# One attention stage of a fused network: its output product cut in two halves, its unit table rewritten, one copy moved ahead of another

## The reference

```python
def _L2_xattn_ref(q, k, v, mask, Wq, Wk, Wv, Wo, bo):       # q = layernorm(x), k = v = ctx_1024
    qh, kh, vh = heads_split(q @ Wq), heads_split(k @ Wk), heads_split(v @ Wv)     # 16 heads of 64
    dots = jnp.einsum('bhid,bhjd->bhij', qh, kh) * 64 ** (-0.5)
    dots = jnp.where(mask[:, None, :, :], mask_value, dots)
    attn = jax.nn.softmax(dots, axis=-1)
    out = jnp.einsum('bhij,bhjd->bhid', attn, vh)
    out = out.transpose(0, 2, 1, 3).reshape(b, n, h * d)
    return out @ Wo + bo
...
    x = x + _L2_xattn_ref(_layernorm(x, axis=-1), ctx_1024, ctx_1024, mask_BxSxS2_bk1, ...)
```

## Time and profile before

| | |
|---|---|
| median of the timed runs | 2631.06 us |
| the profiled execution, and the span of its trace | 2642.36 us, 2640.4 us |
| mean granted TensorE clock over the span | 0.918 |
| TensorE busy over the span | 84% |
| the stage, from its first `score` to its last write to X | 1316.7 to 1961.1 us |
| steps 0 to 7, the first eight | 45.51 us |
| one ordinary block of eight steps (1562.93 to 1602.68) | 39.75 us |
| the eleven blocks of steps 8 to 95 | 442.24 us |

### The profile page before, as it was taken

The page is one execution under the profiler, slowest core; times in us unless marked ns, Lnnn a source line. Parts: engine busy times, 40 slices in busy tenths (PEclk is TensorE's granted clock), DMA queues, the critical chain, the costliest instruction groups (busy, mean ns, idle before and its releaser), DMA issues. The chain is left out here.

```text
span 2640.4 us, 62412 instructions
## 1 busy us (share of the span) xinstructions
PE 2208.6 (84%) x23896; PEld 1460.3 (55%) x23896; DVE 1561.2 (59%) x3648; ACT 1375.1 (52%) x2919; POOL 954.2 (36%) x1066
## 2 busy tenths in 40 slices
PE   4989399599999999868589999999974992899756
PEld 2556255377777777636356666666652551566533
DVE  3666672566665665456766666666665644555463
ACT  2666363355555555334366666666653652566543
POOL 3443222254444544313323233233313742443043
PEclk8999599799999999959799999999986996999967
DMA  5663361300000000010200000000023215333133
GB/s 121 118 115 65 112 212 35 121 17 10 14 14 14 8 14 2 2 33 1 92 8 14 9 14 10 13 14 8 2 69 101 72 57 119 91 74 74 31 106 107
DMA packets 118579, 139.57 MB, mean 53 GB/s; under 512 B 15072, under 2 KB 107184, under 8 KB 118288
## 3 DMA queue, kind: packets, MB, share of 16 engines
q1 hardware_dynamic: 110900, 115.39, 17.0%
q0 software_dynamic: 7392, 20.19, 2.5%
HBM read 93.25 MB, written 17.47 MB: 42 GB/s over the span
## 5 line engine op out<-in xcount | busy, mean ns | idle before, releaser
L899 DVE TENSOR_REDUCE a_mx<-a_pair 112x2 f32<-112x750 f32 x256 | 238.0, 936 | 191.5 <-PE a_pair L968 191.5
L1207 POOL TENSOR_TENSOR a_kp<-a_kp 125x512 f16<-125x512 f32 x192 | 217.6, 1158 | 259.4 <-ACT a_kp L1298 259.4
L308 POOL TENSOR_SCALAR a_P<-a_P,a_inv 112x375 f32<-112x375 f32 x256 | 148.4, 593 | 447.5 <-DVE a_inv L435 447.5
L430 DVE CUSTOM_DVE_ANT_0 a_masked<-a_s,a_mask_add 112x375 f32<-112x375 f32 x256 | 130.1, 546 | 156.2 <-PE a_s L556 156.2
L837 ACT ACTIVATE a_PT<-a_pair 125x672 f32<-125x672 f32 x256 | 186.2, 730 | 66.6 <-PE a_pair L980 61.9
L346 ACT ACTIVATE a_P<-a_masked,a_least 112x375 f32<-112x375 f32 x256 | 153.5, 601 | 81.7 <-DVE a_least L430 81.7
L520 PE MATMUL a_p<-a_kc,a_wk 128*128 128x375 f16 x768 | 147.9, 329 | 21.2 <-DVE a_k L460 10.2
L1341 DVE SCALAR_TENSOR_TENSOR a_k<-a_p,a_k 128x375 f16<-128x375 f32 x128 | 69.3, 547 | 139.2 <-ACT a_k L1254 139.2
L534 PE MATMUL a_p<-a_wv,a_kc 128*125 128x512 f16 x576 | 142.4, 383 | 10.5 <-DVE a_k L460 10.4
L1298 ACT CAST a_kp<-a_kp 125x512 f16<-125x512 f32 x192 | 110.4, 617 | 76.4 <-DVE a_kp L1360 76.4
L1440 PE MATMUL a_p<-a_kc,a_wk 128*128 128x375 f16 x768 | 142.2, 326 | 5.4 <-POOL a_kc L1199 5.4
(11 more groups left out here) (420 smaller groups left out, 5258.8 us busy)
## 6 DMA issues: line engine op xcount, KB each, us to landing
a_kc<-in_ctxT SPq DMA_DIRECT2D x64, 375.0 KB, 4.1
a_k<-a_k_parts SPq DMA_DIRECT2D x192, 93.8 KB
w_stage<-in_L_ffn_W SPq DMA_DIRECT2D x32, 512.0 KB
w_stage<-in_L_ffn_ew SPq DMA_DIRECT2D x16, 512.0 KB, 6.6
w_stage<-expert_rows SPq DMA_DIRECT2D x16, 448.0 KB, 7.6
a_v_in_sb<-in_ctx SPq DMA_DIRECT2D x16, 375.0 KB
a_q<-a_q_parts SPq DMA_DIRECT2D x48, 112.0 KB, 3.7
w_stage<-in_L_ffn_W SPq DMA_DIRECT2D x16, 256.0 KB, 3.9
```

The source lines that it names most:

```text
L308: pool.tensor_scalar(P[:, p % 4, r, :], P[:, p % 4, r, :], inv[:, p % 4, r:r + 1], 1.0, ALU.mult, ALU.mult).then_inc(P_done, 1)
L430: dve.tensor_tensor_reduce(masked[:, p % 2, r, :], s_bank[0:S, r, 0:SK], mask_add[:, b % 2, :], 1.0, 3e38, ALU.add, ALU.min, least[:, p % ...
L899: dve.tensor_reduce(mx[:, b % 2, 2 * pair:2 * pair + 2], pair_bank[slot["score", p]][0:S, :, 0:SK], AX.X, ALU.max).then_inc(max_done, 1)
L1207: pool.tensor_tensor(kp16[:, LO, j, hf, r, :, :].rearrange("p c m -> p (c m)"), kp[:, n % 4, :], kp16[:, HI, j, hf, r, :, :].rearrange("p ...
```

## The change

The `out` unit becomes two, one for each half of the heads: half 0 takes chunks 0 to 3 at place 0 of the next block, half 1 chunks 4 to 7 at its place 4, each of 12 products instead of 24, and each added to X. The `v` units of all batches but the first move to places 5, 6, 7, 1, 2 and 3. With this every place of a block has two units, and places 2 and 6 a `q` unit as third. `parts_of` cuts the units of a step into an early one, a middle and a last. ACT evacuates the early unit ahead of `high_PT` (it came behind it), DVE takes the early unit's low part ahead of `low_PT`, the middle one's at the end of the step, and leaves only the last one to the following step. `invert(s)` moves from step `s + 1` into step `s`. POOL adds the bias to X two steps earlier, and the loop has one step fewer.

```diff
@@ -176,9 +176,11 @@
     INNER = H * HD
     TURN, WEIGH = 2, 3
     NPAIR = B * NP
-    FIRST, LAST = -3, NPAIR + WEIGH + 2
+    FIRST, LAST = -3, NPAIR + WEIGH + 1
     WO_AT = 3
-    V_AT = {-3: (0, 0), -1: (1, 0), 1: (2, 0), 2: (0, 1), 4: (1, 1), 6: (2, 1)}
+    V_FIRST = {-3: (0, 0), -1: (1, 0), 1: (2, 0), 2: (0, 1), 3: (1, 1), 4: (2, 1)}
+    V_AT = {-3: (0, 0), -2: (1, 0), -1: (2, 0), 1: (0, 1), 2: (1, 1), 3: (2, 1)}
+    OUT_AT = {NP: 0, NP + WEIGH + 1: 1}
 
     def units_at(s):
 
@@ -190,9 +192,15 @@
                 found += [("q", 0, t + 3)] if 0 <= t + 3 < C else []
             elif b % GT == 0:
                 found += [("q", b // GT, (t + 26) // 4)] if -26 <= t <= 2 and (t + 26) % 4 == 0 else []
-            found += [("v", b, V_AT[t])] if t in V_AT else []
-            found += [("out", b, 0)] if t == NP + WEIGH + 2 else []
+            v_at = V_AT if b else V_FIRST
+            found += [("v", b, v_at[t])] if t in v_at else []
+            found += [("out", b, OUT_AT[t])] if t in OUT_AT else []
         return found
+
+    def parts_of(s):
+
+        found = units_at(s)
+        return found[:-1][:1], found[1:-1], found[-1:]
 
     steps = range(FIRST, LAST + 1)
     order = [unit for s in steps for unit in units_at(s)]
@@ -322,7 +330,7 @@
                             split_context(b)
                         if t == -4 and b >= 2:
                             make_mask(b)
-                        if t == NP:
+                        if t == NP - 2:
                             pool.tensor_tensor(X[:, b, :], X[:, b, :], bo_bc[:, :], ALU.add).then_inc(biased, 1)
 
             @block.scalar
@@ -369,8 +377,8 @@
 
                 def take_y(b, hf):
                     act.wait_ge(weighed, NP * b + 4 * hf + 4)
-                    if b >= 2 and hf == 0:
-                        act.wait_ge(projected, number["out", b - 2, 0] + 1)
+                    if b >= 2:
+                        act.wait_ge(projected, number["out", b - 2, hf] + 1)
                     act.copy(yT16[:, b % 2, HI, 4 * hf:4 * hf + 4, :],
                              y_bank[hf][:, 0:4 * S].rearrange("p (n s) -> p n s", s=S)).then_inc(y_hi, 1)
 
@@ -392,8 +400,12 @@
                 act.mul(wv16[:, HI, :, :], staged["v"], WS).then_inc(w_hi, 1)
                 high_context(1)
                 for s in steps:
+                    early, middle, last = parts_of(s)
                     if 0 <= s < NPAIR:
                         exponentiate(s)
+                    for unit in early:
+                        if unit[0] != "out":
+                            evacuate(unit)
                     if 0 <= s - TURN < NPAIR:
                         high_PT(s - TURN)
                     if 0 <= s - WO_AT < 4:
@@ -401,7 +413,7 @@
                     p = s - WEIGH - 1
                     if p >= 0 and p % 4 == 3:
                         take_y(p // NP, p % NP // 4)
-                    for unit in units_at(s):
+                    for unit in middle + last:
                         if unit[0] != "out":
                             evacuate(unit)
                     for b in range(2, B):
@@ -483,12 +495,15 @@
                 dve.scalar_tensor_tensor(wv16[:, LO, :, :], staged["v"], WS, wv16[:, HI, :, :], ALU.mult,
                                          ALU.subtract).then_inc(w_split, 1)
                 for s in range(FIRST, LAST + 2):
+                    early, middle, _ = parts_of(s)
                     if 0 <= s < NPAIR:
                         least_of(s)
-                    for unit in units_at(s - 1)[-2:]:
+                    for unit in parts_of(s - 1)[2]:
                         low(unit)
-                    if 0 <= s - 1 < NPAIR:
-                        invert(s - 1)
+                    if 0 <= s < NPAIR:
+                        invert(s)
+                    for unit in early:
+                        low(unit)
                     if 0 <= s - TURN < NPAIR:
                         low_PT(s - TURN)
                     if 0 <= s - WO_AT < 4:
@@ -496,7 +511,7 @@
                     p = s - WEIGH - 1
                     if p >= 0 and p % 4 == 3:
                         low_y(p // NP, p % NP // 4)
-                    for unit in units_at(s)[:-2]:
+                    for unit in middle:
                         low(unit)
                     for g in range(1, G):
                         if s == 32 * (g - 1) + 5:
@@ -535,12 +550,13 @@
                                                wv16[:, z, j, w * 512:(w + 1) * 512],
                                                start=i == j == 0, stop=(i, j) == (2, DC - 1))
                     else:
-                        pe.wait_ge(y_done, 2 * b + 2)
+                        hf, chunks = c, range(4 * c, 4 * c + 4)
+                        pe.wait_ge(y_done, 2 * b + hf + 1)
                         pe.wait_ge(wo_split, 4)
                         for i, (x, z) in enumerate(PARTS):
-                            for c in range(C):
-                                mm = pe.matmul(out[0:S, 0:D], yT16[:, b % 2, x, c, :], wo16[:, z, c, :],
-                                               start=i == c == 0, stop=(i, c) == (2, C - 1))
+                            for j in chunks:
+                                mm = pe.matmul(out[0:S, 0:D], yT16[:, b % 2, x, j, :], wo16[:, z, j, :],
+                                               start=(i, j) == (0, chunks[0]), stop=(i, j) == (2, chunks[-1]))
                     mm.then_inc(projected, 1)
 
                 def score(p):
```

## The result

Four timed runs of the changed kernel gave a median of 2595.53 us (2586.50 to 2597.78); four of the kernel before on the same chip 2632.01 us (2626.16 to 2633.26). The ratio is 0.9857, with a 95% interval from 0.9838 to 0.9875: 36.5 us faster. The profiled execution took 2597.31 us (span 2595.4, mean granted clock 0.917). In its lines, `score` is L572, `turn` L582, `weigh` L598, the products of `k`, `q`, `v` and `out` units L535, L542, L549 and L558.

What follows compares the result with a forecast made beforehand. TensorE was taken to set the pace, losing time in six of eight steps to a bank that DVE empties one step late. The terms sum to 37.1 us, taken from 2631.06 to give 2594 us, range 2583 to 2617.

Steps and rivals of the forecast that it cites:

- steps 0 to 7: Start of the stage: 8.2 us of gaps, about half closed by earlier low parts, 3 us less, from 0 to 6.
- The gapless step: Two-unit step without a TensorE gap: 4.38 us, read off places 1 and 4; 5.56 with a `q` unit.
- the two ends of the block's gain: Gain per block: 2.35 us from gapless step lengths, or 1.72, TensorE's idle time alone, as low end.
- The walk through a step: Two-unit step followed in place 4's times: copy at 3.2 us, low part 3.7, `low_PT` 4.25 to 5.17, `turn` 5.0.
- Two covers: Margins of 0.25 to 0.3 us: `low_PT` ahead of `turn`, and a free bank ahead of `k` at places 0 and 4.
- the ring: Closed chain `turn`, `weigh`, `k`, ACT's copy, DVE's low part, `low_PT`, next `turn`: 4.2 us with semaphores, below TensorE's 4.38.
- the surplus at steps 37 and 69: 5.0 us over eleven blocks, mostly splitting of rows; the `v` unit waits much as before, so no gain counted.
- The last output product: At the stage's end, running alone: 24 products took 4.46 us, halved to 12 they take 2.2.
- Rival (a): DVE arrives late in steps with `low_PT` behind a unit, half the gain left: 2609 us; chance 0.17.
- Rival (b): Gaps only move: TensorE waits at `turn` instead of the units, 0.25 us a step, 2628 us; chance 0.06.
- Rival (c): Slower: the chain through the early unit becomes the period; with 1.0 us more, about 2665 us; chance 0.05.
- The clock: TensorE's granted clock, 1.00 in the block: denser work does not make it fall, and nothing is added for it.

Runs made afterwards that it cites:

- e1_order_alone: New order on ACT and DVE with the unit table and whole output product of the kernel before: 2605.12 us, ratio 0.9903.
- e3_output_whole: Changed kernel without the halving, the output product whole at place 5: 2602.07 us, ratio 0.9892.
- e5_fill_in_ring: Changed kernel plus two DVE memsets of 448 columns between the early unit's low part and `low_PT`: 2663.33 us, ratio 1.0115.
- e10_act_order_old: Changed kernel with ACT's order of before, copying the early unit behind casts and `take_y`, DVE's order as changed: 2624.97 us, ratio 0.9932.
- e9_two_moves: Changed kernel with the split of rows in two halves and, after step 4, the `q` unit last in its step: 2602.38 us, ratio 0.9855.
- e11_only_one_left: Changed kernel with ACT's order of before and DVE's early low part behind `low_PT`, one unit left to the next step: 2616.86 us, ratio 0.9896.

## Why the prediction was right

Predicted 2594 us, measured 2595.53; predicted 37.1 us less, measured 37.7 in the stage and 36.5 between the medians. By the terms of the sum:

| term | predicted | measured |
|---|---|---|
| steps 8 to 95 | 25.9 | 26.4 |
| steps 96 to 103 | 2.7 | 2.4 |
| steps 104 to 119 | 4.8 | 4.6 |
| steps 120 to 124 | -1.8 | -1.9 |
| the end, to the next norm | 2.5 | 2.8 |
| steps 0 to 7 | 3.0 | 4.3 |
| norm to step 0 | 0 | -0.9 |
| sum | 37.1 | 37.7 |

- *The gapless step* was read off two rows and held: 4.38 to 4.43 where I said 4.38, 5.55 for 5.56, a block of 37.48 for 37.40.
- *Of the two ends of the block's gain*, 2.35 and 1.72, the measured 2.27 decides for the first. The stage gained 26.4 us in steps 8 to 95 though only 22.0 were idle: in a step with a gap the busy time is longer too (4.45 us for 4.38 at place 7, with the same products). The Trainium skill (Perfetto Trace Analysis, Identifying the Most-Contended Engine) says that matmul busy time is no good measure of how close a kernel is to its roofline; the rows agree, with 6.7 us less of it for the same 3961 products.
- *The walk through a step* is confirmed instruction by instruction: the copy 3.20 us into the step (predicted 3.2), the low part at 3.72 (3.7), `low_PT` from 4.18 to 5.09 (4.25 to 5.17), `turn` at 5.00 (5.0). Two covers are confirmed by it; the ring's slack of 0.25 came out as 0.25 where no `q` unit hides it. One reading of the prediction is off, without effect on the sum: ACT works 25 us of the 39.75, not 26.
- *Eleven blocks at 2.27* make 25.0 of the 26.4. The other 1.4 is a term that I mis-sized: "I give it nothing" for the surplus at steps 37 and 69. Steps 38 and 70 went from 8.28 and 9.32 us to 6.82 each, 1.27 over a usual 5.55. Their `v` unit does still wait, but half as long. Five other steps whose units stand in the order `k`, `q`, `v` are 0.2 us longer than I had reckoned.
- *Steps 0 to 7* gave 4.3 for my 3.0, with the range of 0 to 6 that I had named.
- *The last output product* took 1.49 us where I said 2.2. Half of 4.46 was the wrong way to it, since I had not looked at the clock in that stretch: 0.62 before, 1.00 after. That the end as a whole came out at 2.8 for my 2.5 is in part luck: this product alone gave 3.0, and the rest of the end lost 0.2, with the other half stretched to 2.24 us by the same lower clock.
- *Rival (a)* fell: no cover was gone. *Rival (b)* fell: `turn` does not wait for `low_PT` in the block. *Rival (c)* was a true mechanism with too little delay. With 0.95 us put into it the kernel is slower than before by 1.15% (0.99 to 1.30): 42.4 us a block reckoned for 1.0 us more, 41.50 measured. That its 2665 us and the measured 2663 are so close is luck: the block came out shorter, and the blocks without a `q` unit, which pay more, make up for it.
- *The clock* stayed 1.00 from step 0 to step 124 with the gaps gone, as with them; in the last stretch it was 0.91, and 0.93 before.

What I did not have: which edit does it. I had treated the early unit as the core. The runs show that leaving one unit instead of two behind `least_of`, with the even table, keeps 31.4 of the 37.7 us; the early unit adds 6.3, `invert` nothing, and the new table without the new order nothing either (-0.6). Leaving one unit instead of two on the old table, without the rest, was not run.

## What to carry to other kernels

Where two engines in strict order empty a bank in two passes, ask for each product which of its predecessors is emptied a step late, read the gapless step's length off a step that has no gap, and multiply: here that predicted 2.35 us a block where the idle time gave 1.72 and 2.27 was measured. An even table of work and an order that empties banks in time are one change in two parts; tried singly, one of them looks worthless. Before moving an instruction ahead of another, close the ring that this makes, add up its durations and compare with the period: a delay of 0.95 us cost 0.06 us a block outside the ring and 4.02 inside it.

## What the runs showed that I had not expected

TensorE's clock at the end of the stage. The last output product follows 1.33 us without a product. Whole, with 24 products, it took 4.46, 4.18 and 4.22 us at a granted clock of 0.62, 0.66 and 0.65 (before, `e1_order_alone`, `e3_output_whole`). Halved, it took 1.49 us in eight of ten kernels (at 1.00 in the changed one), but 2.52 us at 0.56 in `e5_fill_in_ring` and 2.78 us at 0.50 in `e10_act_order_old`. But the halving does not escape the lower clock. In the changed kernel the clock had already fallen and come back when the last half began; the half before it met the lower level:

```profile
1918.78 2.24 PE L558 MATMUL a_p<-a_wo,a_yT 128*112 128x256 f16 x12
```

```profile
1918.78:1921.02 2.24, 2.24 (x16) 2.24 (x15) 0.11 (x1) 0.00 (x0) 0.00 (x0) 0.66 0.04 7
```

The same 12 products took 1.52 us in an ordinary block. In all ten halved kernels this first half took between 2.06 and 2.81 us. So both halves together took 3.73 us in the changed kernel, where the whole took 4.46: the halving brings some of the work out of the low stretch. In each of the thirteen traces the clock is 1.00 up to the last few steps and 0.50 for some microseconds in the last of them, where TensorE has gaps (0.92, 0.92 and 1.54 us, waiting for POOL, ahead of the fall in the changed kernel). When exactly it falls differs from kernel to kernel, and what sets it is not shown.

The phases that the change does not touch do not repeat from one profiled execution to the next. Over the thirteen profiled kernels the first phase took 263.5 to 275.0 us. The last one, the layer with experts, took either 123 to 126 us or 137.5 to 139.4: long in the trace of before, `e9_two_moves`, `e10_act_order_old` and `e11_only_one_left`, short in the changed kernel and the other eight. So the profiled spans of before and after differ by 45.0 us: 37.7 for the stage and 13.3 for this phase, less 5.0 for the first phase and 1.0 for the others. The three experiments among the long ones were timed in one session, in which the kernel before, too, took 2643.91 us and not about 2630. The profiled execution of before stands 11.3 us above its timed median, which this phase would explain; the timed runs have no trace, so that is not shown. The same 55 us of it, counted back from where its products end, in the kernel before and after the change:

```profile
2565.00:2620.00 55.00, 47.96 (x324) 26.10 (x322) 25.85 (x72) 25.64 (x73) 28.58 (x30) 0.88 0.24 71
```

```profile
2520.00:2575.00 55.00, 53.14 (x406) 31.72 (x403) 35.35 (x94) 36.48 (x96) 34.28 (x35) 0.93 0.35 104
```

In the long variant fewer products, a lower transfer rate (71 against 104 GB/s) and a lower granted clock come together; which is the cause stays open. What follows for reading is shown: a difference between two spans is not yet the change's, and the length of the stage itself, which repeated within 0.7 us in three kernels, is the better witness.
